# dt by one softplus of ScalarE between two table loads, with fewer C products on GpSimd, in a selective scan with a mixing layer

## The chip, the cores and the metric

The kernel runs on one core of a Trainium2 chip, in float32 apart from a few bf16 helpers. The metric is the device time of one execution in microseconds (us), the median over several.

## The reference, cut to what matters

The sizes are B=4, L=512, model width 256, inner width 512, 16 states, dt rank 16.

```python
xc = silu(conv4(ctx @ in_proj_w.T) + conv_b)          # u, [B, 512, L]
dt_low, Bm, Cm = split(x_proj_w @ xc)                 # 16, 16 and 16 rows
dt = softplus(dt_proj_w @ dt_low + dt_proj_b)         # [B, 512, L]
state = state * exp(dt * A) + dt * u * B[t]           # one state per channel and n, A = -exp(A_log)
y = sum_n(state * C[t]) + D * u
x = x + (y * silu(layernorm(x))).T
x = x + (sum_r layernorm(x) @ factors[r]) / sqrt(8) + bias
```

## The kernel before, in words

**Tiling.** The 512 channels are four blocks of 128 partitions; with four batches this makes 16 steps, step s holding batch b = s // 4 and channel block k = s % 4. A step handles 16 states as 8 pairs (j = 0 to 7), a pair being one 128 x 1024 tile.

**One pair.** ScalarE makes two decays `exp(dt * A)` into the PSUM tile `dA` (L811, called by `decays`). GpSimd multiplies the spread B rows with `dtu` (L1144) into one of the eight buffers of `h`. VectorE scans (L992). The product with the spread C rows is then made by VectorE (L998), the scan having written over `dA`, or for the pairs named in `POOL_C` by GpSimd (L1137), the scan having written over `h`. TensorE adds the product to the PSUM tile `y` (L534). `dA` has two buffers: the decays of pair j+2 wait until the scan (GpSimd's pairs) or the C product (VectorE's pairs) of pair j is done.

**Order.** Each engine has its own instruction stream, written out by hand with semaphores; the only order between engines comes from these waits. Side work is put into slots: work of slot j stands behind pair j's decays on ScalarE, and behind pair j's scan, ahead of its C product, on VectorE. The slots that matter here on ScalarE: the statistics of the next batch's layer norm (`minus_mean` L709, `var_sum` L715), `silu_batch` (one operation between two table loads, in the steps with k = 2), `gate_batch` (four operations between two table loads, in the steps with k = 0), copies out of PSUM (`conv_out`, `x1_evac`, `t_final_`, `t_xnT_`). On VectorE: the last tap of a convolution (L949, slot 0 of steps 5 to 10), `gate_y` (L1006, slot 1), `add_x1` (L1034, slot 2 or 3).

**dt.** `dt_proj` puts the argument for step s+1 into PSUM one step ahead. ScalarE then makes Relu and Abs (slot 0) and Exp, Square, Abs and Ln (slot 1); VectorE makes a polynomial, a minimum and a sum (L963, L969, L975, slot 3 - k % 2). All use one table set, `natural_log_exp_and_others`. At the step's end GpSimd makes `dtu` (L1130) and resets the first column.

**Start.** In projection, convolution, silu, `x_proj`, the dt of step 0, the first B product by VectorE (L1104), then the steps. Rows B and C are written to DRAM and read back, spread over 128 partitions, in 16 transfers of 512 KB; the last of them is B's pair 0 for step 1.

Of the kernel before, what the change touches and what calls it, by code (L numbers as in the profile page):

```python
# [31 lines left out]
P = 128  # L32
# [15 lines left out]
RAW_STATS = {8: ((12, 5), (12, 6), (12, 7)), 9: ((13, 2), (13, 2), (13, 3)),  # L48
# [6 lines left out]
POLY_BELOW = 2.0 ** -7  # L55
# [3 lines left out]
EARLY_POOL_C = (0, 4)  # L59
EARLY_SUM_ORDER = (1, 0, 2, 3, 5, 4, 6, 7)  # L60
POOL_C = (0, 2, 4)
LAST_POOL_C = (0, 2)
SUM_ORDER = (1, 0, 3, 2, 5, 4, 6, 7)
LAST_SUM_ORDER = (1, 0, 3, 2, 4, 5, 6, 7)
C_LAG = 3
TENSOR_RESIDUAL = (0, 1, 2, 6, 8)
SQ_SCALE = 3.0 ** -0.5
IDLE_FILL = {(0, -1): 14, (0, 3): 3, (0, 6): 3, (1, 3): 6, (2, 3): 3, (3, 3): 6, (4, 1): 5, (5, 6): 3, (6, 1): 2,
             (7, 6): 4, (8, 1): 3, (8, 3): 2, (8, 6): 4, (9, 6): 4, (10, 1): 6, (11, 1): 3, (11, 6): 2, (12, 1): 5,
             (13, 1): 5, (14, 3): 5}  # L70


def build(nc, x, ctxT, w_inT, channel, x_projT, dt_wT, factors, bias, out):
    bc_dram = nc.dram_tensor("bc_scratch", (BATCH, 2 * N, L), F32, kind="Internal").ap()

    with ExitStack() as ctx:
# [6 lines left out]
        def sem(name):  # L83
# [8 lines left out]
        w_in = sb("w_in", [P, CB, DI])  # L92
# [23 lines left out]
        l_dt = sb("l_dt", [P, L])  # L116
        q_dt = sb("q_dt", [P, L])
# [15 lines left out]
        cols = sb("cols", [P, 4])  # L133
        eps_col, sq_col, below_col, above_col = (cols[:, i:i + 1] for i in range(4))
# [47 lines left out]
        d_mm, d_relu, d_abs, d_exp, d_sq, d_far, d_ln, d_poly, d_log, d_dt, d_dtu = (  # L182
            sem(f"d_{n}") for n in ("mm", "relu", "abs", "exp", "sq", "far", "ln", "poly", "log", "dt", "dtu"))
# [51 lines left out]
        def blocks_at(part, s, at):  # L235

            early = {t: ((t + KB, 5), (t + KB, 6), (t + KB, 7), (t + KB + 1, 0), (t + KB + 1, 4),
                         (t + KB + 2, -1), (t + KB + 2, 2)) for t in range(2 * KB)}
# [20 lines left out]
        def on_pool(p):  # L259

            s, j = divmod(p, PAIRS)
            return j in (LAST_POOL_C if s == STEPS - 1 else EARLY_POOL_C if s < KB else POOL_C)

        def sum_order(s):

            return LAST_SUM_ORDER if s == STEPS - 1 else EARLY_SUM_ORDER if s < KB else SUM_ORDER

# [33 lines left out]
        def e_bank(n):  # L301

            return dA[:, 0, 0, :] if n == 0 else work2[:]

# [8 lines left out]
        def _(sp):  # L313
            w_columns = w_inT.rearrange("(c p) e -> p c e", p=P)
            sp.dma_start(ctx_sb[:, 0, :], ctxT[0:P, 0, :]).then_inc(first_ctx_landed[0], 16)
            sp.dma_start(w_in[:, :, 0:P], w_columns[:, :, 0:P]).then_inc(w_in_first, 16)
            sp.dma_start(ctx_sb[:, 1, :], ctxT[P:2 * P, 0, :]).then_inc(first_ctx_landed[1], 16)
            sp.dma_start(chan[:], channel.rearrange("(k p) t -> p k t", p=P)).then_inc(ch_landed, 16)
            sp.dma_start(w_in[:, :, P:DI], w_columns[:, :, P:DI]).then_inc(w_in_rest, 16)
            sp.wait_ge(pads_ready, 1)  # L320
            sp.dma_start(w_x[:], x_projT.rearrange("(k p) e -> p k e", p=P)).then_inc(w_x_landed, 16)
# [90 lines left out]
        def _(pe):  # L412
            def in_proj(bank, k, first=False):
                for c in range(CB):
# [3 lines left out]
                    mm = pe.matmul(bank[:], w_in[:, c, k * P:(k + 1) * P], ctx_sb[:, c, :],  # L418
# [217 lines left out]
            pe.wait_ge(ctx_landed, 16)  # L636
            in_proj(work0, 0)
# [6 lines left out]
            mm.then_inc(b_first, 1)  # L644
            in_proj(work1, 1)
# [18 lines left out]
        def _(act):  # L664
# [87 lines left out]
            def softplus_signs(n):  # L752
                act.wait_ge(d_mm, n + 1)
                if n > 0:
                    act.wait_ge(d_dt, n)
# [3 lines left out]
                act.activation(dt[:, n % 2, :], dt_bank(n)[:], ACT.Relu).then_inc(d_relu, 1)  # L759
                act.wait_ge(d_relu, n)  # L760
                act.activation(dt_bank(n)[:], dt_bank(n)[:], ACT.Abs).then_inc(d_abs, 1)

            def first_abs():

                act.wait_ge(d_mm, 1)
                act.activation(q_dt[:], y[:], ACT.Abs).then_inc(d_abs, 1)
                act.wait_ge(bc_evac, 1)
                act.wait_ge(dtl_evac, 1)

            def softplus_parts(n):  # L770
                act.wait_ge(d_abs, n + 1)
                act.activation(e_bank(n), q_dt[:] if n == 0 else e_bank(n), ACT.Exp, scale=-1.0).then_inc(d_exp, 1)
                act.wait_ge(d_exp, n + 1)
                act.activation(q_dt[:], e_bank(n), ACT.Square, scale=SQ_SCALE, bias=sq_col).then_inc(d_sq, 1)
                act.activation(l_dt[:], e_bank(n), ACT.Abs, bias=below_col).then_inc(d_far, 1)
                act.wait_ge(d_far, n + 1)
                act.activation(l_dt[:], l_dt[:], ACT.Ln, bias=above_col).then_inc(d_ln, 1)
# [47 lines left out]
            def step(s):  # L825
# [5 lines left out]
                for j in range(PAIRS):  # L831
# [7 lines left out]
                    if j == 0 and is_d:  # L839
                        softplus_signs(s + 1)  # L840
                    if j == 1 and is_d:
                        softplus_parts(s + 1)
                    if s == 0 and j == 1:
                        x_in_copy(work1, KB + 1)
                        for i in range(KB):
                            nb(g_r, g_mv, i, g_expv, 1, g_nb)
# [7 lines left out]
                    if j == 2 and s > 0 and s + KB + 1 in TENSOR_CONV:  # L854
                        conv_out(s + KB + 1)
                    if j == (4 if k == 0 and s > 0 else 2) and is_g:
# [5 lines left out]
                    if j == 3 and k == KB - 2 and b + 1 < BATCH:  # L862
# [3 lines left out]
                    if j == (5 if k == 0 and s > 0 else 4 - k % 2) and is_g:  # L866
# [42 lines left out]

            act.preload_act_table_set("silu_and_others")  # L910
            act.wait_ge(ch_landed, 16)
# [3 lines left out]
            for k in range(KB):  # L915
                first_silu(k)
            act.preload_act_table_set("natural_log_exp_and_others")
            x_evac(0)
            act.activation(a_neg[:], a_log, ACT.Exp).then_inc(a_exp, 1)
            first_abs()  # L920
            softplus_parts(0)
            conv_tap(work0, KB)
            lnv(g_r, g_mv, slice(0, KB), g_aggr, KB, g_lnv)
            expv(g_r, slice(0, KB), g_lnv, 1, g_expv)
            act.wait_ge(g_neg, 1)
# [15 lines left out]
        def _(dve):  # L941
# [17 lines left out]

            def softplus_poly(n):  # L960
                dve.wait_ge(d_sq, n + 1)
                dve.wait_ge(d_far, n + 1)
                dve.scalar_tensor_tensor(out=e_bank(n), in0=q_dt[:], scalar=13.0 / 16.0, in1=e_bank(n),  # L963
                                         op0=ALU.add, op1=ALU.mult).then_inc(d_poly, 1)

            def softplus_sum(n):
                dve.wait_ge(d_ln, n + 1)
                dve.wait_ge(d_poly, n + 1)
                dve.tensor_tensor(l_dt[:] if n == 0 else e_bank(n), e_bank(n), l_dt[:], ALU.min).then_inc(d_log, 1)  # L969
                dve.wait_ge(d_log, n + 1)  # L970
                if n == 0:
                    dve.scalar_tensor_tensor(out=dt[:, 0, :], in0=y[:], scalar=0.0, in1=l_dt[:], op0=ALU.max,
                                             op1=ALU.add).then_inc(d_dt, 1)
                    return
                dve.tensor_tensor(dt[:, n % 2, :], dt_bank(n)[:], dt[:, n % 2, :], ALU.add).then_inc(d_dt, 1)  # L975
# [61 lines left out]
            def step(s):  # L1037
                b, k = divmod(s, KB)
                nv = s + KB + 2
                is_c, is_d = nv < STEPS and nv not in TENSOR_CONV, s + 1 < STEPS  # L1040
                for j in range(PAIRS):
                    scan(s, j)

                    if s == 0 and j in (0, 1):
# [28 lines left out]
            dve.memset(sq_col, -0.75 * SQ_SCALE)  # L1073
            dve.memset(below_col, -POLY_BELOW)
            dve.memset(above_col, 1.0 + POLY_BELOW)
            dve.memset(w_dt[:], 0.0)
            dve.memset(bias_row[:], 0.0)
            dve.memset(dt_low[:], 1.0).then_inc(pads_ready, 1)
            for n, i in conv_order[:KB * (TAPS - 1)]:
# [194 lines left out]
```

## Time and profile before

| | us |
|---|---|
| median of 3 runs (lowest, highest) | 489.57 (489.28, 491.35) |
| profiled execution, its own time | 488.93 |
| span of the profiled execution, first to last instruction | 487.1 |
| VectorE busy | 467.9 (96%) |
| GpSimd busy | 448.4 (92%) |
| TensorE matmul busy | 439.7 (90%) |
| ScalarE busy | 349.7 (72%) |

All durations below come from the profiled execution. Its own time is 1.8 above its span, the part outside the first and last instruction. Busy is the time in which an instruction of the engine runs; matmuls overlap, so TensorE's figure is no measure of a full engine. The mean granted TensorE clock is 0.993 of full speed.

### The profile page before, as it was taken

What the parts mean: (1) busy time and instruction counts of PE and PEld (TensorE: products, weight loads), DVE (VectorE), ACT (ScalarE), POOL (GpSimd) and SP (SyncE); (2) the same over time, 40 slices, a digit from 0 to 9 for tenths busy, and PEclk for the clock granted to TensorE, in tenths of its full rate; (3) what the DMA queues carried; (4) which work ended last, traced back from release to release, by engine and by line L of the source; (5) the groups of instructions that cost most, each with busy time, mean ns of one, the idle gap of its engine ahead of it and who ended that gap; (6) DMA issues with size and microseconds to landing.
All of it is one profiled execution on the core that took longest, in us unless ns stands there. A gap on an engine that the chain in (4) does not pass through costs nothing.

```text
span 487.1 us, 4317 instructions
## 1 busy us (share of the span) xinstructions
PE 439.7 (90%) x1139; PEld 187.4 (38%) x1154; DVE 467.9 (96%) x366; ACT 349.7 (72%) x625; POOL 448.4 (92%) x235
## 2 busy tenths in 40 slices
PE   8788897999888969999989899889899798998996
PEld 5233343434333333433434343333434343443432
DVE  4899999999999999999999999999999999999996
ACT  2789655978569869797788977698689885743422
POOL 4379899999899999999999999999999999999982
PEclk9999899999999989999999999999999999999999
DMA  6799744439982000100793000000395000000002
GB/s 190 258 361 340 195 81 99 85 70 225 288 341 86 0 0 0 62 5 1 236 412 114 1 22 1 0 22 1 111 393 237 0 23 22 22 22 22 1 0 86
DMA packets 17872, 53.97 MB, mean 111 GB/s; under 512 B 2724, under 2 KB 3236, under 8 KB 16824
## 3 DMA queue, kind: packets, MB, share of 16 engines
q1 hardware_dynamic: 16696, 45.31, 25.8%
q0 software_dynamic: 1152, 8.39, 8.5%
q8 instruction: 9, 0.15, 0.1%
q14 instruction: 15, 0.12, 0.1%
HBM read 49.24 MB, written 4.46 MB: 110 GB/s over the span
## 4 chain that ended last, share of the span: by engine, by line
POOL 61%; issue 18%; DVE 9%; DMA 5%; PE 3%; SPq 2%; ACT 1%; POOLq 0%; DVEq 0%; ACTq 0%
POOL h L1144 40%; POOL h L1137 15%; DVE dA L992 4%; DMA b_rep<-bc_scratch 4%; POOL dtu L1130 3%; DVE acc L949 2%; DVE h L992 1%; POOL fsum L1170 1%; SPq L351 1%; POOL fsum L1174 1%; PE y L534 1%; SPq L346 1%; PE y L624 1%; DVE h L998 1%; POOL x L1188 1%
## 5 line engine op out<-in xcount | busy, mean ns | idle before, releaser
L1144 POOL TENSOR_TENSOR h<-b_rep,dtu 128x1024 f32<-128x1024 f32 x127 | 302.3, 2449 | 13.2 <-DVE dtu L1100 9.8
L534 PE MATMUL y<-h,ident 128*128 128x512 f32 x508 | 240.3, 607 | 30.0 <-DVE h L998 28.9
L811 ACT ACTIVATE dA<-dt,a_neg 128x512 f32<-128x512 f32 x256 | 165.8, 679 | 88.4 <-DVE h L998 76.0
L992 DVE TENSOR_TENSOR_SCAN dA<-dA,h 128x1024 f32<-128x1024 f32 x85 | 194.1, 2283 | 0.5 <-ACT dA L811 0.5
L534 PEld LDWEIGHTS y<-h,ident 128*128 128x128 f32 x508 | 91.9, 191 | 159.1 <-issue 99.9
L1137 POOL TENSOR_TENSOR h<-h,c_rep 128x1024 f32<-128x1024 f32 x43 | 103.4, 2405 | 5.4 <-DVE h L992 5.3
L998 DVE TENSOR_TENSOR h<-dA,c_rep 128x1024 f32<-128x1024 f32 x84 | 102.3, 1218 | 1.4
L992 DVE TENSOR_TENSOR_SCAN h<-dA,h 128x1024 f32<-128x1024 f32 x43 | 98.0, 2279 | 1.4 <-ACT dA L811 1.4
L418 PE MATMUL work<-ctx_sb,w_in 128*128 128x512 f32 x60 | 28.7, 607 | 1.9 <-DVE x L1034 1.4
L522 PE MATMUL work<-fsum,xnT 128*128 128x512 f32 x64 | 28.8, 592 | 0.0
L949 DVE SCALAR_TENSOR_TENSOR acc<-work,chan,acc 128x511 f32<-128x511 f32 (+2 forms) x30 | 21.5, 729 | 5.2 <-ACT acc L670 5.0
L529 PE MATMUL y<-ones,still 128*128 128x512 bf16 x76 | 20.0, 379 | 0.6
L1130 POOL TENSOR_TENSOR dtu<-dt,u 128x512 f32<-128x512 f32 x15 | 19.8, 1318 | 0.0
L430 PE MATMUL work<-row_b,x 128*128 128x512 f32 (+3 forms) x40 | 18.0, 593 | 1.9 <-ACT row_b L678 1.9
L522 PEld LDWEIGHTS work<-fsum,xnT 128*128 128x128 f32 x64 | 12.2, 190 | 15.3 <-issue 15.3
L418 PEld LDWEIGHTS work<-ctx_sb,w_in 128*128 128x128 f32 x60 | 11.2, 194 | 17.2 <-issue 14.9
L565 PE MATMUL y<-u,diag_d 128*128 128x512 f32 x32 | 17.4, 626 | 0.0
L445 PE MATMUL work<-dt_low,w_dt 32*128 32x512 f32 x30 | 16.8, 640 | 0.0
L529 PEld LDWEIGHTS y<-ones,still 128*128 128x128 bf16 x88 | 8.6, 98 | 16.0 <-issue 10.3
L709 ACT ACTIVATE xnT<-x 128x512 f32<-128x512 f32 x13 | 8.1, 620 | 9.0 <-DVE x L1027 9.0
L498 PE MATMUL work<-fsum,x 128*128 128x512 f32 x32 | 14.5, 595 | 0.0
L670 ACT ACTIVATE acc<-work,chan 128x512 f32<-128x512 f32 x10 | 7.7, 766 | 7.3 <-PE work L418 7.3
(141 smaller groups left out, 441.5 us busy)
## 6 DMA issues: line engine op xcount, KB each, us to landing
b_rep<-bc_scratch SPq DMA_DIRECT2D x32, 512.0 KB, 9.2
c_rep<-bc_scratch SPq DMA_DIRECT2D x32, 512.0 KB, 8.8
fsum<-factors POOLq DMA_DIRECT2D x8, 1024.0 KB, 8.1
x<-x SPq DMA_DIRECT2D x4, 1024.0 KB, 7.9
out<-x SPq DMA_DIRECT2D x16, 256.0 KB, 2.0
ctx_sb<-ctxT SPq DMA_DIRECT2D x3, 512.0 KB, 5.7
ctx_sb<-ctxT SPq DMA_DIRECT2D x2, 256.0 KB, 3.6
w_in<-w_inT SPq DMA_DIRECT2D x1, 384.0 KB, 4.3
```

The lines of the kernel that those rows point to most:

```text
L418: mm = pe.matmul(bank[:], w_in[:, c, k * P:(k + 1) * P], ctx_sb[:, c, :], start=(c == 0), stop=(c == CB - 1))
L430: mm = pe.matmul(work1[:, i:L], tap_diag[:, k, TAPS - 1 - i, :], x_in[:, 0:L - i], start=(i == 0), stop=(i == TAPS - 1))
L522: pe.matmul(work1[:], xnT[:, k, :], fsum[:, k, :], start=(k == 0), stop=False)
L529: pe.matmul(y[:], still[:], ones[:], start=False, stop=False)
L534: mm = pe.matmul(y[:], ident[:], h[:, (s * PAIRS + j) % H_RING, i, :], start=False, stop=(j == sum_order(s)[-1] and i == 1))
L811: act.activation(dA[:, j % 2, i, :], dt[:, k % 2, :], ACT.Exp, scale=a_neg[:, k, 2 * j + i:2 * j + i + 1]).then_inc(exp_done, 1)
L949: dve.scalar_tensor_tensor(out=acc[:, k, i:L], in0=bank[:, 0:L - i], scalar=cw[:, k, TAPS - 1 - i:TAPS - i], in1=acc[:, k, i:L], op0=ALU.m ...
L992: dve.tensor_tensor_scan(pair if on_pool(s * PAIRS + j) else decay, decay, pair, 0.0, ALU.mult, ALU.add).then_inc(scanned, 1)
L998: dve.tensor_tensor(h[:, (s * PAIRS + j) % H_RING], dA[:, j % 2], c_rep[:, j], ALU.mult).then_inc(mulc, 1)
L1130: pool.tensor_tensor(dtu[:, k % 2, :], dt[:, k % 2, :], u[:, n // KB % 2, k, :], ALU.mult).then_inc(d_dtu, 1)
L1137: pool.tensor_tensor(h[:, p % H_RING], h[:, p % H_RING], c_rep[:, p % PAIRS], ALU.mult).then_inc(pmulc, 1)
L1144: pool.tensor_tensor(h[:, (s * PAIRS + j) % H_RING], b_rep[:, j], dtu[:, k % 2, :].unsqueeze(1).to_broadcast([P, 2, L]), ALU.mult).then_in ...
```

## The change

- **dt**: `softplus` takes the place of `softplus_signs`, `softplus_parts`, `softplus_poly` and `softplus_sum`: a load of the set `softplus`, one activation from PSUM to `dt`, a load of the old set. It stands in slot 2 of steps 0 to 14. VectorE has no part in it.
- **C products**: GpSimd makes those listed per step in `POOL_C`, 31 in place of 43; the twelve others, pair 4 of steps 1, 3, 4, 5, 6 and 8 to 14, go to VectorE. The order of TensorE's sums follows.
- **Slots on ScalarE**: `gate_batch` and `silu_batch` from slot 3 to slot 4; `conv_out` from 2 to 3; `minus_mean` from slot 2 to 3 (from 4 to 5 where k = 0); `var_sum` to slot 3 (k = 0: slot 5 as before). The statistics of output block 9 and one turn of TensorE move by a slot.
- **Start**: weights come in a layout with longer runs per partition; two loads are issued from ScalarE's queue in place of SyncE's; the exp of `A_log` is made first; the two matmuls that spread B's first pair stand ahead of the next in projection; two of the four statistics and the aggregation of batch 0's layer norm move from ahead of the first scan to behind it, and the ScalarE work that needs them to slots 0 and 1 of step 0.
- **TensorE's idle fill**: 53 matmuls in place of 88.

```diff
-POOL_C = (0, 2, 4)          # steps 0-3: (0, 4), last step: (0, 2)
+POOL_C = ((0, 4), (0,), (0, 2), (0,), (0, 2), (0, 2), (0, 2), (0, 2, 4), (0, 2), (0, 2), (0, 2), (0, 2), (0, 2), (0, 2),
+          (0, 2), (0, 2))
+SOFTPLUS_SLOT = 2
...
+            act.dma_start(w_in[:, 0].rearrange("p c e -> p (c e)"), w_inT[:, 0:DM]).then_inc(w_in_first, 16)
+            act.dma_start(chan[:].rearrange("p k t -> p (k t)"), channel).then_inc(ch_landed, 16)
...
+            def softplus(n):
                 act.wait_ge(d_mm, n + 1)
                 if n >= 2:
                     act.wait_ge(exp_done, (n - 1) * (2 * PAIRS))
                     act.wait_ge(dt_reset, n - 1)
+                act.activation(dt[:, n % 2, :], dt_bank(n)[:], ACT.Softplus).then_inc(d_dt, 1)
...
-                    if j == 0 and is_d:
-                        softplus_signs(s + 1)
-                    if j == 1 and is_d:
-                        softplus_parts(s + 1)
+                    if j == SOFTPLUS_SLOT and is_d:
+                        act.preload_act_table_set("softplus")
+                        softplus(s + 1)
+                        act.preload_act_table_set("natural_log_exp_and_others")
+                    if s == 0 and j == 0:
+                        conv_tap(work0, KB)
                     if s == 0 and j == 1:
                         x_in_copy(work1, KB + 1)
+                        lnv(g_r, g_mv, slice(0, KB), g_aggr, KB, g_lnv)
+                        expv(g_r, slice(0, KB), g_lnv, 1, g_expv)
...
-                    if j == 3 and k == KB - 2 and b + 1 < BATCH:
+                    if j == 4 and k == KB - 2 and b + 1 < BATCH:
                         act.preload_act_table_set("silu_and_others")
                         silu_batch(b + 1)
...
-                    if j == 3 - k % 2 and is_d:
-                        softplus_poly(s + 1)
-                        softplus_sum(s + 1)
```

## Rows read from the trace of the kernel before

**Rows 1.** Busy times, step 8: stretch, length, PE, PEld, DVE, ACT, POOL busy.

```profile
253.17:282.34 29.17, 25.90 (x67) 10.76 (x68) 28.48 (x23) 25.08 (x43) 27.96 (x15) 1.00 0.23 83
```

**Rows 2.** Groups by line, GpSimd (POOL): busy us, mean ns, then its idle.

```profile
L1137 POOL TENSOR_TENSOR h<-h,c_rep 128x1024 f32<-128x1024 f32 x43 | 103.4, 2405 | 5.4 <-DVE h L992 5.3
```

**Rows 3.** Timeline of VectorE (DVE), step 8, pairs 0 to 6: start, duration.

```profile
253.17 2.28 DVE L992 TENSOR_TENSOR_SCAN h<-dA,h 128x1024 f32<-128x1024 f32 x1
...
256.01 2.28 DVE L992 TENSOR_TENSOR_SCAN dA<-dA,h 128x1024 f32<-128x1024 f32 x1
...
259.92 2.28 DVE L992 TENSOR_TENSOR_SCAN h<-dA,h 128x1024 f32<-128x1024 f32 x1
...
262.70 2.28 DVE L992 TENSOR_TENSOR_SCAN dA<-dA,h 128x1024 f32<-128x1024 f32 x1
...
267.01 1.22 DVE L998 TENSOR_TENSOR h<-dA,c_rep 128x1024 f32<-128x1024 f32 x1
268.75 2.29 DVE L992 TENSOR_TENSOR_SCAN h<-dA,h 128x1024 f32<-128x1024 f32 x1 [0.52 <-ACT dA L811]
270.95 2.27 DVE L992 TENSOR_TENSOR_SCAN dA<-dA,h 128x1024 f32<-128x1024 f32 x1
273.26 1.22 DVE L998 TENSOR_TENSOR h<-dA,c_rep 128x1024 f32<-128x1024 f32 x1
274.40 2.29 DVE L992 TENSOR_TENSOR_SCAN dA<-dA,h 128x1024 f32<-128x1024 f32 x1
```

**Rows 4.** VectorE's scans as a group: what they waited for (us, times).

```profile
  ACT dA L811: 1.8, 5
```

**Rows 5.** Timeline of ScalarE (ACT), step 8, from pair 3's decays on.

```profile
260.04 1.30 ACT L811 ACTIVATE dA<-dt,a_neg 128x512 f32<-128x512 f32 x2 [1.72 <-DVE h L998]
261.28 0.58 ACT L799 ACTIVATE x<-work 128x512 f32<-128x512 f32 x1
261.87 1.28 ACT L899 ACT_TABLE_LOAD   x1
263.17 2.93 ACT L705 ACTIVATE gate<-x,g_r 128x512 f32<-128x512 f32 x4
266.12 1.28 ACT L901 ACT_TABLE_LOAD   x1
267.41 1.30 ACT L811 ACTIVATE dA<-dt,a_neg 128x512 f32<-128x512 f32 x2
```

**Rows 6.** Groups by line and shape, ScalarE: busy us, mean ns, then its idle.

```profile
L759 ACT ACTIVATE dt<-work 128x512 f32<-128x512 f32 x15 | 8.7, 580 | 2.0 <-PE work L445 1.9
L715 ACT ACTIVATE xnT<-x,g_mv 128x512 f32<-128x512 f32 x12 | 8.5, 709 | 0.0
...
L697 ACT ACTIVATE u<-acc 128x2048 f32<-128x2048 f32 x3 | 5.7, 1914 | 0.0
```

**Rows 7.** Timeline of all engines, from the start to step 1's first scan.

```profile
20.45 1.98 PE L418 MATMUL work<-ctx_sb,w_in 128*128 128x512 f32 x4
...
22.37 1.98 PE L642 MATMUL dA<-dt_low,ident 64*128 64x512 f32 x4
...
26.27 1.22 DVE L1104 TENSOR_TENSOR h<-dA,dtu 128x1024 f32<-128x1024 f32 x1
...
27.80 2.29 DVE L992 TENSOR_TENSOR_SCAN h<-dA,h 128x1024 f32<-128x1024 f32 x1 [0.31 <-ACT dA L811]
...
37.72 1.23 DVE L998 TENSOR_TENSOR h<-dA,c_rep 128x1024 f32<-128x1024 f32 x1
...
52.52 2.38 POOL L1144 TENSOR_TENSOR h<-b_rep,dtu 128x1024 f32<-128x1024 f32 x1 [1.87 <-issue]
...
56.87 2.28 DVE L992 TENSOR_TENSOR_SCAN h<-dA,h 128x1024 f32<-128x1024 f32 x1
```

**Rows 8.** Step 0's eight spread C transfers: time from issue to landing.

```profile
DMA to landing us min/median/max: 5.9/11.1/21.1
```

**Rows 9.** Timeline of VectorE, step 13, slot 1.

```profile
398.07 0.69 DVE L1006 TENSOR_TENSOR yg<-y,gate 128x512 f32<-128x512 f32 x1 [0.86 <-PE y L534]
```

More of the change, by code:

```diff
@@ L132, in build @@
         t_r = sb("t_r", [P, 3, KB])
-        cols = sb("cols", [P, 4])
-        eps_col, sq_col, below_col, above_col = (cols[:, i:i + 1] for i in range(4))
+        eps_col = sb("eps_col", [P, 1])[:]
         dA = ps("dA", [P, 2, 2, L])
@@ L235, in blocks_at @@
         def blocks_at(part, s, at):
-            early = {t: ((t + KB, 5), (t + KB, 6), (t + KB, 7), (t + KB + 1, 0), (t + KB + 1, 4),
+            early = {t: ((t + KB, 5), (t + KB, 6), (t + KB, 7), (t + KB + 1, 1), (t + KB + 1, 4),
                          (t + KB + 2, -1), (t + KB + 2, 2)) for t in range(2 * KB)}
@@ L261, in on_pool @@
             s, j = divmod(p, PAIRS)
-            return j in (LAST_POOL_C if s == STEPS - 1 else EARLY_POOL_C if s < KB else POOL_C)
+            return j in POOL_C[s]
         def sum_order(s):
-            return LAST_SUM_ORDER if s == STEPS - 1 else EARLY_SUM_ORDER if s < KB else SUM_ORDER
+            return SUM_ORDERS[POOL_C[s]]
         def tensor_convs(n):
@@ L853, in step @@
                         conv_out(KB + 1)
-                    if j == 2 and s > 0 and s + KB + 1 in TENSOR_CONV:
+                    if j == 3 and s > 0 and s + KB + 1 in TENSOR_CONV:
                         conv_out(s + KB + 1)
-                    if j == (4 if k == 0 and s > 0 else 2) and is_g:
+                    if j == (5 if k == 0 else 3) and is_g:
                         act.wait_ge(x_landed, (b + 2) * 16)
@@ L861, in step @@
                         x1_evac(s - 1)
-                    if j == 3 and k == KB - 2 and b + 1 < BATCH:
+                    if j == 4 and k == 0:
+                        act.preload_act_table_set("silu_and_others")
+                        gate_batch(b)
+                        act.preload_act_table_set("natural_log_exp_and_others")
+                    if j == 4 and k == KB - 2 and b + 1 < BATCH:
                         act.preload_act_table_set("silu_and_others")
@@ L865, in step @@
                         act.preload_act_table_set("natural_log_exp_and_others")
-                    if j == (5 if k == 0 and s > 0 else 4 - k % 2) and is_g:
+                    if j == (5 if k == 0 else 3) and is_g:
                         var_sum(g_mv, b + 1, k, g_scratch, g_mean, s + 1, g_var)
@@ L916, in _ @@
                 first_silu(k)
+            act.preload_act_table_set("softplus")
+            x_evac(0)
+            softplus(0)
             act.preload_act_table_set("natural_log_exp_and_others")
[L918 to L925, printed above, removed]
+            act.wait_ge(bc_evac, 1)
+            act.wait_ge(dtl_evac, 1)
             act.wait_ge(a_ready, 1)
@@ L1039, in step @@
                 nv = s + KB + 2
-                is_c, is_d = nv < STEPS and nv not in TENSOR_CONV, s + 1 < STEPS
+                is_c = nv < STEPS and nv not in TENSOR_CONV
                 for j in range(PAIRS):
                     scan(s, j)
+                    if s == 0 and j == 0:
+                        for i in range(2, KB):
+                            stats(g_stat, 0, i, g_bn)
+                        for i in range(KB):
+                            aggr(g_mv, g_stat, i, g_bn, i + 1, g_aggr)
+                        dve.wait_ge(g_aggr, KB)
+                        dve.tensor_scalar(g_mv[:, :, 0], g_mv[:, :, 0], -1.0, None, ALU.mult).then_inc(g_neg, 1)
                     if s == 0 and j in (0, 1):
```

103 lines of the change are left out of this document (23 added, 80 removed).

## The prediction

> **What bounds the kernel now.** I read the page's busy times first: VectorE runs for 96% of the span, GpSimd for 92%. By step it is the same: in step 8 VectorE is busy for 28.48 of 29.17 us and GpSimd for 27.96, ScalarE for 25.08 [rows 1]. So two engines are nearly full, and a third is fuller than its 72% over the span suggests. The timeline of VectorE then tells what a slot is worth; I count from one start to the next, since neighbours overlap. A pair whose C product is GpSimd's takes 270.95 - 268.75 = 2.20 us, one with its own C product 274.40 - 270.95 = 3.45 [rows 3]. VectorE's scans waited for ScalarE's decays only five times, 1.8 us in all [rows 4], one of them 0.31 at the start [rows 7]. VectorE thus sets the end, and whatever leaves it shortens the kernel, as long as ScalarE's decays stay in time. They can run ahead of the scans by two pairs at most, for `dA` has two buffers. That is the reading on which all below rests.
>
> **VectorE's part.** Its three operations for dt: in step 8 pair 3's scan starts at 262.70 and its C product at 267.01, 4.31 later; in pair 5, with nothing between, it is 273.26 - 270.95 = 2.31 [rows 3]. They cost 2.00, in steps 1 to 14 that is 28.0. The twelve C products taken over cost 3.45 - 2.20 = 1.25 each, 15.0. Net **-13.0**.
>
> **GpSimd's part.** It loses 12 x 2.41 = 28.9 us [rows 2], one product in most steps: step 8 goes from 27.96 to 25.6, below what VectorE needs (29.17 - 0.52 - 2.00 + 1.25 = 27.9). I count nothing; its cover is VectorE, and it runs ahead up to the ring of eight.
>
> **ScalarE's part.** Six operations go, one and two table loads come. The new block: a load holds ScalarE for 263.17 - 261.87 = 1.30 and 267.41 - 266.12 = 1.29 [rows 5]. Softplus isn't in the trace; Relu of the same tile takes 0.58 [rows 6], a gate activation 2.93 / 4 = 0.73 [rows 5]. I take 0.60, as its operands are Relu's, so 3.2 for the block. In sum ScalarE has no more work than before. But the block stands in one piece between the decays of pairs 2 and 3, and the next burst (gate or silu) now follows in slot 4. So I walk step 8 from its first scan at 0. VectorE, if never kept waiting, starts the scans at 2.84, 6.75, 9.53 as before [rows 3], then 12.98 and 16.43. ScalarE may make pair 2's decays when scan 0 ends, at 2.3; 1.25 for them and 3.2 for the block lead to 6.8; pair 3's wait for pair 1's C product, 260.04 - 253.17 = 6.87 [rows 5]; to 8.1; the copy of slot 3 to 8.7; pair 4's wait for scan 2, over at 6.75 + 2.28 = 9.03, and end at 10.3; the gate burst takes 267.41 - 261.87 = 5.54, to 15.85; pair 5's decays let its scan start 268.75 - 267.41 = 1.34 later, at 17.2 [rows 5]. That is 0.8 late, where the old order was 0.52 late. So dt no longer costs VectorE anything by itself, but the burst does. The others in the same way:
> - Step 4: no convolution tap ahead of scan 1 (-0.64 for VectorE); scan 5 wanted at 15.8, possible at 16.8: 1.0.
> - Step 12: likewise, with a copy of 0.5 more behind the gate burst: 17.3 against 15.8, 1.5.
> - Step 2: slot 3 holds two copies out of PSUM and the two statistics, each of the four between 0.5 and 0.71 [rows 6], 2.4 in all, then the silu burst of 1.30 + 1.91 + 1.29 = 4.5 [rows 5, 6]. Pair 4's decays start at 6.8 + 1.25 + 2.4 = 10.45, scan 5 can start at 10.45 + 1.3 + 4.5 + 1.34 = 17.6; VectorE, with neither residual nor tap, wants 15.2: 2.4.
> - Steps 6 and 10: 17.6 against 16.45, 1.15 each.
> - Odd steps: no burst; with the block and 2.4 of slot 3, pair 4's decays start at 10.45 and its scan can start at 11.8, and VectorE wants it at 11.8 to 13.0. Nothing.
>
> Sum 8.0, against 1.8 - 0.3 = 1.5 before: **+6.5**.
>
> By the rows the engine goes on at once behind a load: the next instruction starts 1.29 or 1.30 after it [rows 5]. The Trainium skill, ScalarE: Activation LUTs, section What ACT_TABLE_LOAD costs, says otherwise: 1.28 us for the load and 1.38 for a drain, 2.66 for each switch of set, which speaks against this change. By it the block would be 5.9 instead of 3.2. The trace agrees with its figure for the load and shows no such drain in the gap.
>
> **The start.** The matmuls that spread B's first pair now stand ahead of an in projection, 22.37 - 20.45 = 1.9 earlier, and dt comes after one operation, so the product of L1104 (26.27) and the first scan (27.80) move some 4 us forward [rows 7]. The statistics moved behind the first scan take back about 2. What follows hangs on transfers which leave no earlier than before, give or take 0.4: pair 2's C product started at 37.72 [rows 7]; its rows were issued fourth of eight, with a median of 11.1 from issue to landing [rows 8], so they landed about 37, and it can't start much sooner. From there to the first scan of step 1 took 56.87 - 37.72 = 19.15; now 17.15 without dt. But the gate burst of step 0 stands behind pair 4's decays: from the start of pair 2's C product it is 1.2 + 1.25 + 5.54 + 1.34 = 9.4 to scan 5, and VectorE wants it after 1.13 + 3.45 + 2.20 = 6.8. 2.6 late, so 36.6 + 17.15 + 2.6 = 56.4, or 55.0 if the rows land early. The last spread B, used at 52.52, allows no less than 54.9. I take 56.1: **-0.8**, bounds 0 and -2.0.
>
> **TensorE.** The 35 fill matmuls left out stand where the engine waits anyway (step 8: 25.90 busy of 29.17 [rows 1]) and cost nothing. In step 13 `gate_y` waited 0.86 for it [rows 9], because GpSimd's late pair 4 held up the sums ahead of the mixing layer. That pair is now VectorE's, so **-0.9**. DMA issues moved to ScalarE's queue stand where it has nothing to do: 0.
>
> **Sum.** -13.0 + 6.5 - 0.8 - 0.9 = -8.2. Span 487.1 - 8.2 = 478.9; with the 1.8 around it the profiled execution would be 480.8. The median before is 0.6 above its profiled execution: **481.4**.
>
> **Rivals.**
> - *ScalarE keeps up.* If the slots hold less than I put into them, the bursts cost VectorE nothing: -13.0 - 1.5 - 2.0 - 0.9 = -17.4, 472.2. For it: 72% busy over the span, with the walk's slots filled by estimate. Against it: decays can't be made earlier than two pairs ahead, and in step 8 the old order already missed by 0.52 [rows 3].
> - *The bursts cost twice my sum.* A burst that ends late delays pair 6's decays too, when slot 5 is full; 8.0 more and nothing at the start: 490.2, no change that can be told. Step 8's slot 5 holds a copy and three statistics, some 2.5, which nearly fill a pair's 3.45 with its decays.
> - *Clock or order of TensorE.* With less fill it idles longer while VectorE waits, its clock falls, and `gate_y` waits a microsecond more in five or six steps: 487. Against it: the 3.3 us that it has to spare in step 8 [rows 1].
> - *A change of set to softplus costs double* (slower). If each of the two loads took 1.3 more than the rows' 1.3, the block would be 5.8. Steps with an even k have no cover, 8 x 2.6 = 21; in the 7 odd ones half is covered, 9: 511. From 1.3 more per block on, the gain is gone and 2.5 with it. Against it: neither of the two loads in [rows 5] shows it, and 0.04 is for a set that behaves otherwise. (The Trainium skill, ScalarE: Activation LUTs, What ACT_TABLE_LOAD costs, has about this time, 2.66 for each switch.)
> - *The change isn't what it says*, say more loads are put in: would show at once, included in the last.
>
> **Chances.** Forecast 0.55 (477 to 486); ScalarE keeps up 0.19; twice the bursts 0.12; TensorE 0.06; double loads 0.04; something else, slower, 0.04. A change below 0.5% (2.4 us, 487.1 to 492.0) can't be told from none. Faster: 0.55, 0.19, and the better part of TensorE's case, 0.79. Same 0.12, slower 0.09. The range goes from the first rival to the second: 473 to 489, leaving out 0.05 below and 0.12 above.
>
> **What would show it.** VectorE busy about 450; its scans waiting 8 to 11 us for decays, nearly all at pair 5 of the steps with even k, step 2 and step 0 most; none in odd steps; pair 3 never late; table loads 1.28 with no gap behind; Softplus 0.6; GpSimd idle some 20 us more; first scan near 23.5, first scan of step 1 near 56. Wrong would be: waits of scan 3 (the block is longer), waits of `gate_y` for TensorE (clock), waits for B products (GpSimd).

## The result, and the profile after

| | before | after |
|---|---|---|
| median of 4 runs each (lowest, highest), us | 490.15 (489.28, 491.35) | 482.65 (482.47, 482.95) |
| ratio with its 95% interval | | 0.9846 [0.9821, 0.9871] |
| span of the profiled execution, us | 487.1 | 480.7 |
| waits of VectorE's scans for decays, us | 1.8 | 11.1 |

The changed kernel is 7.5 us faster; the forecast was 481.4. Two things make this figure uncertain by a microsecond or two. The kernel before had medians of 489.26 to 489.30 in three later comparisons, of 9 to 11 runs each, so 0.9 of the 7.5 may be its own spread. And the changed kernel had 484.38 when it was run again (after_again, below), 4.9 less than the 489.30 beside it.

The page's busy times of the changed kernel:

```profile
PE 432.1 (90%) x1119; PEld 185.3 (39%) x1119; DVE 453.5 (94%) x327; ACT 344.7 (72%) x578; POOL 420.6 (88%) x223
```

VectorE lost 14.4 us of work (467.9 before) and GpSimd 27.8 (448.4 before), but the span lost only 6.4. The groups by line show the new work (columns as in [rows 2]):

```profile
L776 ACT ACTIVATE dA<-dt,a_neg 128x512 f32<-128x512 f32 x256 | 166.0, 681 | 92.9 <-DVE h L952 76.2
L952 DVE TENSOR_TENSOR h<-dA,c_rep 128x1024 f32<-128x1024 f32 x96 | 117.1, 1220 | 2.4 <-DMA c_rep<-bc_scratch 0.3
L1086 POOL TENSOR_TENSOR h<-h,c_rep 128x1024 f32<-128x1024 f32 x31 | 74.5, 2403 | 22.3 <-DVE h L946 22.3
L805 ACT ACT_TABLE_LOAD x15 | 19.2, 1283 | 0.3
L807 ACT ACT_TABLE_LOAD x15 | 19.2, 1283 | 0.3
L742 ACT ACTIVATE dt<-work 128x512 f32<-128x512 f32 x15 | 9.0, 598 | 0.2
```

L742 is the softplus, 0.60 us, and each load 1.28: thirty loads, 38.4 us of ScalarE, have come in. The last column tells the price: VectorE's scans (L946) waited

```profile
  ACT dA L776: 11.1, 10
  POOL h L1093: 0.5, 1
```

for decays ten times, against five times and 1.8 before [rows 4]. Where this happens can be read in step 8, on the timeline of VectorE, whose rows answer to [rows 3],

```profile
249.57 2.28 DVE L946 TENSOR_TENSOR_SCAN h<-dA,h 128x1024 f32<-128x1024 f32 x1
...
252.41 2.29 DVE L946 TENSOR_TENSOR_SCAN dA<-dA,h 128x1024 f32<-128x1024 f32 x1
...
256.32 2.28 DVE L946 TENSOR_TENSOR_SCAN h<-dA,h 128x1024 f32<-128x1024 f32 x1
...
259.10 2.29 DVE L946 TENSOR_TENSOR_SCAN dA<-dA,h 128x1024 f32<-128x1024 f32 x1
...
262.56 2.29 DVE L946 TENSOR_TENSOR_SCAN dA<-dA,h 128x1024 f32<-128x1024 f32 x1
...
266.83 2.30 DVE L946 TENSOR_TENSOR_SCAN dA<-dA,h 128x1024 f32<-128x1024 f32 x1 [0.72 <-ACT dA L776]
...
270.75 2.30 DVE L946 TENSOR_TENSOR_SCAN dA<-dA,h 128x1024 f32<-128x1024 f32 x1 [0.37 <-ACT dA L776]
```

and of ScalarE, whose rows answer to [rows 5]:

```profile
253.20 1.28 ACT L805 ACT_TABLE_LOAD   x1
254.50 0.60 ACT L742 ACTIVATE dt<-work 128x512 f32<-128x512 f32 x1
255.11 1.28 ACT L807 ACT_TABLE_LOAD   x1
256.44 1.30 ACT L776 ACTIVATE dA<-dt,a_neg 128x512 f32<-128x512 f32 x2
257.68 0.57 ACT L764 ACTIVATE x<-work 128x512 f32<-128x512 f32 x1
258.63 1.30 ACT L776 ACTIVATE dA<-dt,a_neg 128x512 f32<-128x512 f32 x2 [0.38 <-DVE h L946]
259.95 1.28 ACT L833 ACT_TABLE_LOAD   x1
261.25 2.93 ACT L690 ACTIVATE gate<-x,g_r 128x512 f32<-128x512 f32 x4
264.20 1.28 ACT L835 ACT_TABLE_LOAD   x1
265.50 1.30 ACT L776 ACTIVATE dA<-dt,a_neg 128x512 f32<-128x512 f32 x2
```

The first four scans come one after the other with no wait, at 0, 2.84, 6.75 and 9.53 us of the step, although ScalarE spends 3.2 us on softplus and its loads: when it began with them, at 253.20, the decays of pairs 1 and 2 were made, and pair 2's scan started only at 256.32. Then the gate burst, 259.95 to 265.50, is longer than that lead, and pair 5 starts 0.72 late. Pair 6 starts 0.37 late; its decays stood behind the statistics of slot 5.

The executions are best compared from the first scan of step 1 on (windows, columns as in [rows 1]; the row of before first, then that of after):

```profile
56.87:487.10 430.23, 391.91 (x1008) 167.11 (x1020) 420.12 (x304) 311.40 (x562) 411.22 (x205) 1.00 0.28 89
```

```profile
56.38:480.70 424.32, 383.18 (x986) 165.11 (x986) 408.79 (x274) 307.65 (x522) 383.04 (x193) 1.00 0.29 90
```

VectorE's work falls by 420.12 - 408.79 = 11.33 us there, its idle time rises from 10.11 to 15.53, by 5.42: 5.91 gained. Ahead of that window 56.87 - 56.38 = 0.49 is gained, in all 6.4.

### The profile page after: what moved, and what is told of

It reads as the page before. It is cut to its first block, busy times and chain, and to the rows that moved or that the text cites. A ratio compares the mean times of both kernels' runs of the same rounds, so it can differ in the third digit from the quotient of the medians.

```text
span 480.7 us, 4118 instructions
## 1 busy us (share of the span) xinstructions
PE 432.1 (90%) x1119; PEld 185.3 (39%) x1119; DVE 453.5 (94%) x327; ACT 344.7 (72%) x578; POOL 420.6 (88%) x223
## 4 chain that ended last, share of the span: by engine, by line
POOL 53%; issue 20%; DVE 11%; ACT 6%; PE 4%; DMA 4%; SPq 1%; POOLq 0%; DVEq 0%; ACTq 0%
POOL h L1093 40%; POOL h L1086 9%; DVE dA L946 7%; POOL dtu L1079 3%; DMA c_rep<-bc_scratch 2%; PE y L519 2%; DVE acc L920 2%; ACT dA L776 1%; DMA chan<-channel 1%; DVE h L952 1%; PE work L415 1%; POOL fsum L1123 1%; DVE h L946 1%; ACT gate L690 0%; SPq L331 0%
## 5 line engine op out<-in xcount | busy, mean ns | idle before, releaser
L519 PE MATMUL y<-h,ident 128*128 128x512 f32 x508 | 236.5, 602 | 34.9 <-DVE h L952 33.0
L946 DVE TENSOR_TENSOR_SCAN dA<-dA,h 128x1024 f32<-128x1024 f32 x97 | 221.8, 2287 | 11.6 <-ACT dA L776 11.1
L952 DVE TENSOR_TENSOR h<-dA,c_rep 128x1024 f32<-128x1024 f32 x96 | 117.1, 1220 | 2.4 <-DMA c_rep<-bc_scratch 0.3
L1086 POOL TENSOR_TENSOR h<-h,c_rep 128x1024 f32<-128x1024 f32 x31 | 74.5, 2403 | 22.3 <-DVE h L946 22.3
L946 DVE TENSOR_TENSOR_SCAN h<-dA,h 128x1024 f32<-128x1024 f32 x31 | 70.6, 2279 | 0.1
L403 PE MATMUL work<-ctx_sb,w_in 128*128 128x512 f32 x60 | 30.6, 644 | 0.3 <-DMA w_in<-w_inT 0.2
L514 PE MATMUL y<-ones,still 128*128 128x512 bf16 x53 | 13.9, 379 | 0.0
```

What stands on the lines that cost most here:

```text
L403: mm = pe.matmul(bank[:], w_in[:, k, c, :], ctx_sb[:, c, :], start=(c == 0), stop=(c == CB - 1))
L519: mm = pe.matmul(y[:], ident[:], h[:, (s * PAIRS + j) % H_RING, i, :], start=False, stop=(j == sum_order(s)[-1] and i == 1))
L946: dve.tensor_tensor_scan(pair if on_pool(s * PAIRS + j) else decay, decay, pair, 0.0, ALU.mult, ALU.add).then_inc(scanned, 1)
L952: dve.tensor_tensor(h[:, (s * PAIRS + j) % H_RING], dA[:, j % 2], c_rep[:, j], ALU.mult).then_inc(mulc, 1)
L1086: pool.tensor_tensor(h[:, p % H_RING], h[:, p % H_RING], c_rep[:, p % PAIRS], ALU.mult).then_inc(pmulc, 1)
```

## The experiments

Three questions: do the table loads cost time where they stand; was the shift of C products needed, with GpSimd freed of nothing else; and which waits of the changed kernel can be had back. "Step 1 to end" is the stretch from the first scan of step 1 to the end of the profiled execution, 424.3 us in the changed kernel in both of its profiled executions. The median also holds the start, which differed by up to 2 us between executions of one program (last part of this section), and only the last four runs (best, after_again, fill_as_before, spread_late) were made beside the changed kernel itself. So where a median and this stretch disagree, the stretch says more about the edit.

### The loads

**no_loads.** Relu, which is in the loaded set, in place of softplus in the blocks of steps 0 to 14, and no loads there. The dt of steps 1 to 15 is then another function; the work of the other engines stays.

```diff
-                        act.preload_act_table_set("softplus")
                         softplus(s + 1)
-                        act.preload_act_table_set("natural_log_exp_and_others")
```

> The changed kernel with Relu in place of Softplus in slot 2 and without the 30 loads around it, so dt of steps 1 to 15 is wrong and 38.4 us of loads leave ScalarE. Theory A (the block of 3.2 us lies in a gap of ScalarE; what keeps VectorE waiting is the gate or silu burst alone, held back by the release of the two dA buffers): step 2's wait falls by 0.5, step 4's by 0.2, the small waits of 0.3 in steps 7, 8 and 11 go, all others stay: 1.0 to 2.0 us faster than the changed kernel's 482.65, so 480.7 to 481.7. Rival B (the loads set the bursts' lateness): the waits of 11.1 us go for the most part, 473 to 475.

Measured: 480.96 us, ratio to before 0.9836 [0.9814, 0.9857]. ScalarE was busy for 305.2 us, 39.5 less than in the changed kernel, and step 1 to end took 422.3, only 2.0 less. The scans still waited for it:

```profile
  ACT dA L776: 8.8, 8
```

With one wait of 0.7 for GpSimd, in step 8, the scans wait for 9.5 us in place of 11.6, which is the 2.0. So 38.4 us of loads are worth 2 us. Most of the waits belong to the other bursts (gate and silu), not to these loads.

**loads_doubled.** The same pair of loads once more ahead of each block, so that a block is 2.6 us longer. This is the rival of the double loads, built.

```diff
                         act.preload_act_table_set("softplus")
+                        act.preload_act_table_set("natural_log_exp_and_others")
+                        act.preload_act_table_set("softplus")
                         softplus(s + 1)
                         act.preload_act_table_set("natural_log_exp_and_others")
```

> The changed kernel with two loads more in each of the 15 blocks of steps 0 to 14 (2.6 us each, 38.6 in all); the output stays. Theory A (the gap ahead of pair 3 is used up): even steps with a burst lose 2.0 to 2.6 each, 17 in all; the others are late at pair 3 by 1.2 to 3.0, 16 in all; 510 to 518. The prediction's own sum had 30 for this (half of the odd steps covered), 512. Rival (ScalarE is idle for 28% of the span and absorbs it): under 490.

Measured: 514.5 us, ratio 1.0502 [1.0479, 1.0525]; step 1 to end 454.3, 30.0 more than in the changed kernel. The scans' waits:

```profile
  ACT dA L776: 38.7, 22
```

A first 38.4 us of loads cost 2, the next 38.6 cost 30. The price of a load is not its length, but what of the block sticks out of the lead that the two buffers of `dA` allow. The prediction gave 511 for blocks 2.6 longer, 21 of its 30 us in the steps with an even k and 9 in the others. The sum came out, the split did not: the waits of the scans grew by 15.4 in the even steps (nothing in step 0, 1.1 in step 14) and by 13.1 in the odd ones, where less was covered than the half it had assumed.

### The C products

**c_as_before.** The changed kernel with the 43 C products of before on GpSimd.

```diff
-POOL_C = ((0, 4), (0,), (0, 2), (0,), (0, 2), (0, 2), (0, 2), (0, 2, 4), (0, 2), (0, 2), (0, 2), (0, 2), (0, 2), (0, 2),
-          (0, 2), (0, 2))
+POOL_C = ((0, 4),) * 4 + ((0, 2, 4),) * 11 + ((0, 2),)
```

> The changed kernel with the 43 C products on GpSimd as before, so VectorE has 12 products less (15.0 us) and GpSimd 12 more (28.9). Theory A (GpSimd then is the bound: it works on without a gap from the last spread B of the start on, 52.1, and needs 409 us to its last B product and 17 us follow): not under 478.7, and with odd steps waiting for it 480 to 485. Rival (VectorE alone sets the end, as the prediction reads the profile before): 467 to 472.

Measured: 486.18 us, ratio 0.9941 [0.9919, 0.9962]; step 1 to end 427.2, 2.9 more than in the changed kernel. The median is 1.2 above the 480 to 485 that were expected. VectorE has 15 us less to do, and none of it arrives. In the middle of this kernel (138 to 280 us) the windows show, for PE, PEld, DVE, ACT and POOL,

```profile
138.00:280.00 142.00, 127.76 (x305) 53.93 (x309) 131.21 (x89) 116.14 (x197) 141.31 (x70) 0.94 0.24 93
```

GpSimd busy for 141.31 of 142.00 us: it is the bound. Its lateness reaches VectorE by a detour (groups, idle before them):

```profile
L945 DVE TENSOR_TENSOR_SCAN dA<-dA,h 128x1024 f32<-128x1024 f32 x85 | 194.5, 2288 | 22.3 <-ACT dA L775 19.9 <-POOL h L1092 2.3
L775 ACT ACTIVATE dA<-dt,a_neg 128x512 f32<-128x512 f32 x256 | 165.7, 680 | 91.5 <-DVE h L951 58.1 <-DVE h L945 19.7 <-POOL dt L1080 13.5
```

The scans name ScalarE, but ScalarE waited 13.5 us for GpSimd's reset of `dt` (L1080), which stands behind GpSimd's products. The shift of C products is worth these 2.9 us: it relieves the engine that would otherwise be the bound.

**c_alone.** The kernel before with only the new `POOL_C` and its orders of sums.

> The kernel before with only the C products moved (31 on GpSimd in place of 43) and dt as before. VectorE is full, so each of the 12 costs its 1.25 us: 490.15 + 15 = 505, bounds 502 to 506. Rival (GpSimd was the bound, as the chain of waits of before says with its 61%): 480 to 490.

Measured: 504.33 us, ratio 1.0308 [1.0291, 1.0325], 15.1 slower than before for twelve products that were priced at 15.0. The price of 1.25 us each on VectorE is right, and the relief of GpSimd alone is worth nothing. The two parts of the change depend on each other: the shift alone loses 15.1, the rest of the change without it gains 3.1, both gain 7.5 in the first comparison and 4.9 in the second.

### The waits that are left

**gate_split.** The gate burst in two halves, each between loads of its own: two activations in slot 4 of the steps with k = 0, two in slot 0 of the next step. Eight more loads.

```diff
-                    if j == 4 and k == 0:
+                    if (j, k) in ((4, 0), (0, 1)):
                         act.preload_act_table_set("silu_and_others")
-                        gate_batch(b)
+                        gate_batch(b, (0, 1) if k == 0 else (2, 3))
```

(`(j, k)` is slot and channel block.)

> The changed kernel with the gate burst in halves, two activations between two loads each: blocks 0 and 1 in slot 4 of the steps with k = 0, blocks 2 and 3 in slot 0 of the step after; 8 loads more. Theory A (a burst is hidden up to about 4.2 us, what two pairs of 3.45 leave after the decays of one and the way to the scan): the waits at pair 5 of steps 4, 8 and 12 go (0.9, 0.7, 1.3), step 0's falls from 2.6 to 1.1, and scan 1 of steps 1, 5, 9, 13 is late by 1.05, 0.4, 0.4, 1.05: 2.0 us faster, 480.6, bounds 479.5 to 482. Rival (more loads, 10.3 us, cost what they take): 485 to 492.

Measured: 482.54 us, 0.9848 [0.9828, 0.9869]: 1.9 above what was expected and outside the bounds. Against the 482.65 of the first comparison nothing is gained, against the 484.38 of after_again 1.8. The waits of steps 4, 8 and 12 were gone, with that of step 0 cut from 2.57 to 1.16. New ones of 1.22 came in scan 1 of steps 1 and 13, the one for GpSimd in step 13 grew from 0.47 to 0.71, and a wait of 1.27 for C rows stood in step 0 (0.31 in the changed kernel's first profile, 1.13 in after_again's). Step 1 to end took 423.9, 0.4 less, and step 0 lost 1.4 of its wait. The second half stands ahead of pair 1's decays, and where the lead is short there, the wait is moved and not removed.

**stats_behind.** In the steps with k = 2 the two statistics go from slot 3 to slot 5, behind the silu burst, as they do where k = 0.

```diff
-                    if j == (5 if k == 0 else 3) and is_g:
+                    if j == (5 if k in (0, 2) else 3) and is_g:
```

> The changed kernel with the two statistics of the next batch's norm and one copy moved in steps 2, 6 and 10 from slots 3 and 4 to slot 5, behind the silu burst. Same work. Theory A (what stands ahead of the burst delays it once the block has used up the gap): step 2's wait falls from 2.3 to 1.05, those of steps 6 and 10 from 1.1 to 0, 3.4 us faster: 479.2, bounds 478 to 480.5. Rival (only the burst's length counts): 482.6.

Measured: 480.37 us, 0.9817 [0.9795, 0.9839]; step 1 to end 421.5, 2.8 less than in the changed kernel (3.4 expected). The wait in step 2 fell from 2.28 to 1.00, in step 6 from 1.12 to 0.16, in step 10 from 1.12 to 0.50 (both now at pair 6). ScalarE in step 2, from slot 3 to the burst's end:

```profile
92.13 0.67 ACT L671 ACTIVATE acc<-work,chan 128x512 f32<-128x512 f32 x1
92.70 0.58 ACT L773 ACTIVATE x<-work 128x512 f32<-128x512 f32 x1
93.18 1.30 ACT L778 ACTIVATE dA<-dt,a_neg 128x512 f32<-128x512 f32 x2
94.49 1.28 ACT L839 ACT_TABLE_LOAD   x1
95.78 1.91 ACT L684 ACTIVATE u<-acc 128x2048 f32<-128x2048 f32 x1
97.71 1.28 ACT L841 ACT_TABLE_LOAD   x1
99.01 1.30 ACT L778 ACTIVATE dA<-dt,a_neg 128x512 f32<-128x512 f32 x2
```

The work of slot 3 holds pair 4's decays for 93.18 - 92.13 = 1.05 us, where it held them for 93.70 - 91.33 = 2.37 in the changed kernel; of those 1.32 the wait of scan 5 lost 1.28. This shows the mechanism of the step-2 term: it is the work of slot 3 plus the burst that decides when scan 5 may start.

**both.** The last two together.

> Both edits together, the halved gate burst and the statistics behind the silu burst. They touch different steps, so the gains add: 5.4 us, 477.2, bounds 475.5 to 480. If something else in the chain takes over (GpSimd, TensorE), less than the sum of the two single runs.

Measured: 479.81 us, 0.9799 [0.9776, 0.9823]; step 1 to end 421.0. Within the bounds, 2.6 above the value expected, and not to be told from stats_behind.

**slot1.** The softplus block one slot earlier, from step 1 on, for a longer lead ahead of the burst.

> The changed kernel with the softplus block in slot 1 in place of slot 2, except in step 0. Theory A: pair 3's decays come out of the block's shadow by 0.6 us in the steps without a convolution tap: step 2 gains 0.5, step 4 0.2, the 0.3 of step 11 goes; 0.5 to 1.5 faster, 481.2 to 482.2. Rival (any shift of the block moves the bursts as much): up to 3 faster or slower.

Measured: 483.27 us, 0.9863 [0.9843, 0.9884], outside the 481.2 to 482.2 that were expected; step 1 to end 422.9, 1.4 less, as expected, with step 2's wait at 1.70 in place of 2.28. New waits came in step 13, 0.28 for decays and 0.34 for TensorE, and step 1 began 0.9 later than in the changed kernel's first profile. The median shows no gain; the stretch from step 1 on does.

**best.** stats_behind, with the gate burst halved only in batches 1 and 2, where the halves had brought no new waits.

> The changed kernel with the statistics behind the silu burst (steps 2, 6, 10) and the gate burst halved only where the second half found room, in batches 1 and 2 (steps 4 and 5, 8 and 9). Theory A: on top of the statistics' gain (2.3 measured of 3.4 expected) the waits of 0.9 in step 4 and of 0.7 and 0.4 in step 8 go and nothing comes for them: 2.0 us below the version with the statistics alone (480.4), so 478.4, bounds 477.5 to 480. Rival (a loss of VectorE's waits is taken back later, as in the run with all four halved): 480 to 482.

Measured: 479.78 us, 0.9806 [0.9784, 0.9827]. The changed kernel itself was run beside it once more (**after_again**, below): 484.38. So best is 4.6 us faster than the changed kernel and 9.5 faster than before. Step 1 to end 419.6, 4.75 less than after_again and 1.9 less than stats_behind, as expected. In the median best is only 0.6 below stats_behind, and the intervals overlap. The waits left:

```profile
  ACT dA L778: 6.2, 7
  POOL h L1095: 0.5, 1
```

### The start, the fill, and the spread between runs

**after_again.** The changed kernel, unchanged, beside the next two and best.

> The changed kernel itself beside the other three, so that they are compared on one chip: 482.65 within 0.7.

Measured: 484.38 us (482.98 to 485.52), 0.9894 [0.9875, 0.9914]. This is 1.7 above the 482.65 of the first comparison, and the two intervals of the ratio do not meet. The scans' waits were the same to 0.1 us and step 1 to end took 424.35 against 424.32. All of the difference was ahead of that: the first scan of step 1 started at 58.35 in place of 56.38.

The traces say where it arose. The rows of B and C are first written to DRAM, and the transfers that read them back leave when the write has landed. The write was issued at 19.49 and 19.75; it took 2.0 us to land in the first profile and 3.6 in this one, so the first of those transfers left at 21.50 and at 23.35:

```profile
21.50 0.34 SPq L331 DMA_DIRECT2D b_rep<-bc_scratch  x1
```

```profile
23.35 0.34 SPq L331 DMA_DIRECT2D b_rep<-bc_scratch  x1
```

Pair 2's C product then waited for its rows, 0.31 us in the first profile (its line is below) and 1.13 here:

```profile
38.49 1.23 DVE L952 TENSOR_TENSOR h<-dA,c_rep 128x1024 f32<-128x1024 f32 x1 [1.13 <-DMA c_rep<-bc_scratch]
```

It started 38.49 - 36.53 = 1.96 later, and that is the whole difference. From this product to the first scan of step 1 it is 19.84 to 19.86 us in all ten profiled executions of this family in which step 0 has the whole gate burst. Leaving out spread_late, the nine others begin step 1 at 56.4 to 56.7 where the write took 1.9 or 2.0 us (three), at 57.2 to 57.3 where it took 2.2 to 2.5 (three), and at 58.35 to 58.9 where it took 3.6 to 3.8 (three).

**fill_as_before.** The changed kernel with the 88 fill matmuls of before.

> The changed kernel with the 88 fill matmuls of before in place of 53. The prediction costs the fill at nothing: within 0.7 us of the changed kernel; the granted clock rises from 0.989 to 0.99 or more. Rival (less fill lets the clock fall and TensorE hold up the gate): 1 to 4 us faster.

Measured: 483.25 us, 0.9880 [0.9861, 0.9898], which overlaps with after_again; step 1 to end 424.35, the same. Fewer fill matmuls cost nothing and give nothing, as forecast. The clock did not rise with more of them: 0.988, against 0.989 and 0.993 in the two profiles of the changed kernel.

**spread_late.** The two matmuls that spread B's first pair behind the next in projection, as before.

```diff
+            pe.wait_ge(ctx_landed, 16)
+            in_proj(work0, 0)
             pe.wait_ge(ident_ready, 1)
             pe.wait_ge(bc_evac, 1)
             for i in range(2):
...
             mm.then_inc(b_first, 1)
-            pe.wait_ge(ctx_landed, 16)
-            in_proj(work0, 0)
```

> The changed kernel with the two matmuls that spread B's first pair behind the next in projection again, as before. Theory (the start is set by the landing of the spread C rows and by step 0's gate burst): the first scan comes 1 to 2 us later than 24.7, the first scan of step 1 stays at 56.4 to 57.5, and the time stays within 0.7 us. Rival (the first scan's time carries through): 1 to 2 us slower.

Measured: 485.16 us (484.2 to 487.83), 0.9910 [0.9893, 0.9928], 0.8 above after_again in the median and overlapping with it; the profiled executions differ by 3.3 us. There the first scan started at 28.07 (24.18 in after_again) and that of step 1 at

```profile
61.70 2.28 DVE L946 TENSOR_TENSOR_SCAN h<-dA,h 128x1024 f32<-128x1024 f32 x1
```

against 58.35; from there to the end it was 424.3 again. This is the slowest of the six executions, the only one above 485.9. So the 3.9 us by which the first scan is late are carried to the end of step 0, less 0.5. Both figures are outside what was expected (a first scan at 25.7 to 26.7, step 1 at 56.4 to 57.5). My theory, that step 0 is held by the landing of its C rows and not by its first scan, falls for this execution: no product waited for C rows there. Two things had come together. The four matmuls of the in projection, now ahead of the spread, ran at the low clock, 3.39 us in place of 1.98, and a small operation of VectorE took 2.35 us in place of 0.17 (both are in the last section). Without these 3.6 us pair 2's C product could have started at 38.3 in place of 41.84, which is an estimate; that is no later than the 38.5 to 39.0 at which it started in the executions with as late a write. The theory holds for both profiles of the changed kernel, where the product waited. In the first:

```profile
36.53 1.23 DVE L952 TENSOR_TENSOR h<-dA,c_rep 128x1024 f32<-128x1024 f32 x1 [0.31 <-DMA c_rep<-bc_scratch]
```

Both chains are close, and which comes last changes from one execution to the next.

## Why the prediction was right

The mechanism was as forecast: VectorE is the bound and is relieved by 13 us, and ScalarE's bursts take half of it back. Term by term, in the profiled execution:

- **VectorE's own work, -13.0.** From step 1 to the end the gain was 5.9, and the waits below account for +7.0, +0.5 and -0.9; what remains is -5.9 - 6.6 = -12.5. It shows step by step: less the waits, each of the twelve steps that took a C product over became 0.6 to 0.9 us shorter (2.00 - 1.25 = 0.75 forecast), and steps 2 and 7, which took none over, 1.85 and 2.02 (2.00 forecast). In step 2 GpSimd's product is pair 2's in place of pair 4's, which the list of the change leaves out. c_alone confirms the 15.0 for the C products directly.
- **Softplus block, 3.2 us taken.** 256.44 - 253.20 = 3.24, with 0.60 for softplus, as forecast. By the Trainium skill, ScalarE: Activation LUTs, section What ACT_TABLE_LOAD costs, a switch is 2.66 with its drain. The trace agrees with its 1.28 for the load and not with the drain: the next instruction stands 1.30 and 1.33 behind the start of the load. loads_doubled shows about what the page's figure would have meant for this kernel, whose blocks it makes 2.6 longer: 514.5.
- **The walk of step 8.** Forecast: scans at 2.84, 6.75, 9.53, 12.98, 17.2. Measured: 2.84, 6.75, 9.53, 12.99, 17.26. Pair 3's and pair 4's decays were forecast at 6.87 and 9.03 and started at 6.87 and 9.06. A walk of this kind can be this exact since it adds only durations and starts that the trace before holds.
- **Bursts, 8.0 in six steps.** The forecasts for steps 2, 4, 6, 8, 10, 12 and what was measured: 2.4 and 2.28; 1.0 and 0.94; 1.15 and 1.12; 0.8 and 0.72; 1.15 and 1.12; 1.5 and 1.34. Sum 7.5. Missed were three small waits that the walk ended before or called nothing: pair 6 of step 8, 0.37, and the odd steps 7 and 11, 0.34 and 0.28. With them 8.5 against 1.5 before: +7.0 in place of +6.5. The one in step 11 is at pair 3, a wait that the prediction had named as a sign of being wrong, since it means that the block itself was late; it is 0.28 in one step of fifteen. A part of the rival that priced the bursts twice (pair 6 held by a full slot 5) is thus there, but worth 0.37 and not 8.
- **The start, -0.8.** Measured -0.5. Pair 2's C product was forecast at 36.6 and came at 36.53, and from it to the first scan of step 1 I had 19.75 and it was 19.85; that gives 56.4, and I had shaded it to 56.1. The first scan itself came at 24.66, not 23.5. Step 0's burst wait was forecast at 2.6 and was 2.57. The mechanism is shown: what follows hangs on the landing of the C rows. That the sum came so near is luck, for it depends on how long the write of the rows took: 2.5 us in the profile of before and 2.0 in the first one of the changed kernel. With 3.6 us, in after_again, the same term is 58.35 - 56.87 = +1.5, outside its bounds of 0 and -2.0, and the mean of the nine executions above is 57.5, +0.6.
- **Step 13, -0.9.** `gate_y` no longer waits for TensorE. But the scan of pair 4 now waited 0.47 for a B product of GpSimd, whose engine had itself stood for ScalarE's statistics. Waits for B products were another sign of being wrong. On the timeline, GpSimd and then the scan:

```profile
397.79 1.27 POOL L1137 TENSOR_TENSOR x<-x,row_b 128x512 f32<-128x512 f32 x1 [5.00 <-ACT xn L700]
...
401.49 2.30 DVE L946 TENSOR_TENSOR_SCAN dA<-dA,h 128x1024 f32<-128x1024 f32 x1 [0.47 <-POOL h L1093]
```

  I had priced the shift of these statistics by a slot at nothing. In a span with GpSimd at 88% it held for all steps but this one. In no_loads, where these statistics end 0.6 us earlier in the step, this wait is gone.
- **Fill, 0, and GpSimd's relief, 0.** fill_as_before and c_alone show both.

In sum the span was forecast at 478.9 and is 480.7: 0.3 at the start, 0.5 in VectorE's own work, 0.5 in the bursts, 0.5 for GpSimd. Of the rivals, ScalarE keeping up would have needed a kernel without bursts; even with no loads around softplus 8.8 us of waits stay.

**What stays open.** The ratio to before was 0.9846 in one comparison and 0.9894 in another. The profiled executions place that difference in the time that the write of the rows took to land. Why it took 2.0 us in one execution and 3.6 in another, no run shows, nor whether the executions without a profile differ by it. Of the start, only the place of the spread matmuls was taken back in a run of its own; the new layout of the weights, the loads issued from ScalarE's queue and the moved statistics were not, and the shift of the gate and silu bursts from slot 3 to slot 4 was not tested apart from softplus.

## What to carry to other kernels

Work on an engine at 72% is nearly free only in pieces shorter than its lead; with two buffers that is about one pair here, so write down for each slot when the next buffer is wanted and when it can be ready, and move small work that nobody waits for behind the burst. Trading table loads for vector work pays exactly as long as the block fits: the first 38 us of loads cost 2, the next 38 cost 30. When two engines are both over 90%, as here, taking work off one may need the other relieved in the same edit, and each half tried alone can look like a loss or a small gain. When an edit is worth a few microseconds, run the kernel that it starts from beside it: the changed kernel's own medians were 1.7 apart.

## What the hardware did that I had not expected

**TensorE's clock at the start differs between executions of one program.** The window from 24 to 28 us (length, PE busy, granted clock, DMA share, GB/s), in the changed kernel's first profile and then in that of after_again:

```profile
24.00:28.00 4.00, 4.00 (x6) 0.50 0.89 264
```

```profile
24.00:28.00 4.00, 4.00 (x10) 1.00 0.90 236
```

That is the 1.2 GHz level in the one and 2.4 in the other, with the same matmuls ahead. The eight matmuls of the next in projection took 6.31 us and 3.70. In both the engine had idled for 0.86 us ahead of the two matmuls of `dt_proj` (at 19.55 and 19.81) and had worked without a pause since. It cost nothing that shows here, as the first scan of step 1 came earlier in the execution with the low clock (56.38 and 58.35): pair 2's C product waited for its rows in both.

**A small operation of VectorE stood while GpSimd multiplied.** The scaling of 128x4 elements (L1004), in the changed kernel, in after_again and in spread_late:

```profile
28.44 0.17 DVE L1004 TENSOR_SCALAR g_mv<-g_mv 128x4 f32<-128x4 f32 x1
```

```profile
27.97 1.79 DVE L1004 TENSOR_SCALAR g_mv<-g_mv 128x4 f32<-128x4 f32 x1
```

```profile
31.77 4.96 POOL L1093 TENSOR_TENSOR h<-b_rep,dtu 128x1024 f32<-128x1024 f32 x2 [1.72 <-DMA b_rep<-bc_scratch]
...
31.85 2.35 DVE L1004 TENSOR_SCALAR g_mv<-g_mv 128x4 f32<-128x4 f32 x1
```

In the first, GpSimd was idle from 27.8 to 29.4. In the second a B product of GpSimd ran from 27.32 to 29.72, and the operation ended at 29.76; in the third two of them ran from 31.77 on, and it ended at 34.20, about the end of the first. So 0.17 us of work took up to 2.35, ahead of the second scan. The other profiled executions of this family agree: it took 0.17 in the four where GpSimd was idle or within 0.1 us of its product's end, 0.73 to 0.77 in three and 2.16 to 2.19 in two, and in these five it ended 0.02 to 0.04 after GpSimd's product. The scans, 2.27 to 2.30 us throughout, show nothing of it.
